# Four attention layers on one core: layers 0 and 1 as one list of steps, two gates where two barriers stood

## The reference, cut to what matters

```python
def _L0(x, mask, kv, kv_mask, ...):        # x: 8 x 256 x 512, 16 heads of 16
    q, k, v = Wq x + bq, Wk kv + bk, Wv kv + bv
    attn = softmax(q k / 4 + mask)
    mean, ex2 = attn @ v, attn @ (v * v)
    std = sqrt(relu(ex2 - mean * mean))
    return (instance_norm(x) * std + mean) * mask
def _L1(x, latents, attention_mask, ...):  # latents: layer 0's result
    h = concatenate([x, latents])          # 512 keys, 256 queries, 16 heads of 32
    q = latents @ q_w + q_b;  k, v = h @ kv_w + kv_b
    o = softmax(q k / 32 + mask) @ v @ out_w + out_b + latents
    return gelu(rmsnorm(o) @ mlp_w1 + mlp_b1) @ mlp_w2 + mlp_b2 + latents
```

## Time and profile before

| | us |
|---|---|
| median of three executions | 3299.74 (3284.89 to 3302.26) |
| the profiled execution | 3297.55 |
| its span in the trace | 3295.8 |
| TensorE busy | 2809.2 |
| VectorE busy | 1824.8 |
| ScalarE busy | 1338.8 |
| GpSimd busy | 881.5 |

### The profile page before, as it was taken

How to read it: one execution, slowest core, us unless ns; L and a number is a source line. 1 busy time by engine, 2 the same in 40 slices (tenths; PEclk the granted TensorE clock), 3 DMA queues, 4 the chain that set the end, 5 groups by cost and what they waited for, 6 DMA issues and landing times. The chain is left out here.

```text
span 3295.8 us, 41359 instructions
## 1 busy us (share of the span) xinstructions
PE 2809.2 (85%) x14624; PEld 1317.3 (40%) x14624; DVE 1824.8 (55%) x4498; ACT 1338.8 (41%) x2342; POOL 881.5 (27%) x722
## 2 busy tenths in 40 slices
PE   4988888867999999989999999985668888888895
PEld 1222222224555555556555545542222333333332
DVE  3777777713433433212555665567867776667641
ACT  0566665642333333322333333322215544554562
POOL 1577777752444444310010000001110010101000
PEclk7999999978999999899999999988678899999997
DMA  4444444320002000122323232333333232323210
GB/s 99 102 100 102 102 99 102 67 95 23 27 30 92 28 27 24 65 63 56 67 53 69 57 70 52 70 63 86 67 82 87 69 76 59 89 52 77 66 34 20
DMA packets 182335, 219.93 MB, mean 67 GB/s; under 512 B 40840, under 2 KB 135664, under 8 KB 175984
## 3 DMA queue, kind: packets, MB, share of 16 engines
q1 hardware_dynamic: 170064, 189.74, 25.0%
q0 software_dynamic: 6016, 20.98, 1.9%
q10 hardware_dynamic: 6048, 6.56, 0.6%
HBM read 146.90 MB, written 51.64 MB: 60 GB/s over the span
## 5 line engine op out<-in xcount | busy, mean ns | idle before, releaser
L1260 DVE TENSOR_REDUCE l_M<-PS 128x1 f32<-128x512 f32 x512 | 330.2, 681 | 168.3 <-PE PS L722 167.9
L1480 DVE TENSOR_REDUCE l_M<-PS 128x1 f32<-128x512 f32 x512 | 334.8, 684 | 139.1 <-PE PS L967 136.2
L1199 ACT ACTIVATE l_P<-PS 128x512 f32<-128x512 f32 x512 | 286.3, 599 | 255.3 <-PE PS L977 237.3
L1563 POOL TENSOR_TENSOR l_S<-l_P 128x512 f32<-128x512 f32 x256 | 326.0, 1305 | 62.0 <-ACT l_P L1050 62.0
L1050 ACT ACTIVATE l_P<-PS 128x512 f32<-128x512 f32 x512 | 276.3, 598 | 134.0 <-PE PS L731 133.5
L967 PE MATMUL PS<-l_KS,l_QS 97*128 97x512 bf16 x512 | 205.4, 412 | 102.9 <-DVE l_M L1480 71.7
L1319 DVE TENSOR_REDUCE l1a_M<-PS 128x1 f32<-128x512 f32 x256 | 158.9, 683 | 201.5 <-PE PS L784 201.5
L1164 ACT ACTIVATE l_P<-l_P 128x1024 f32<-128x1024 f32 x128 | 135.3, 1057 | 304.9 <-DVE l_P L1400 304.7
L1386 DVE CUSTOM_DVE_ANT_0 l_JK<-PS,l_MK 128x256 f32<-128x256 f32 x512 | 195.6, 420 | 102.1 <-PE PS L897 99.9
L722 PE MATMUL PS<-l_KS,l_QS 97*128 97x512 bf16 x512 | 202.5, 406 | 57.7 <-DMA l_KS<-l_MB 19.5
L612 PE MATMUL PS<-l_YT,l_w_mlp_w 128*128 128x256 f32 x1024 | 238.6, 390 | 5.2 <-ACT l_YT L1126 5.1
(11 more groups left out here) (244 smaller groups left out, 4639.8 us busy)
## 6 DMA issues: line engine op xcount, KB each, us to landing
l_QS<-q_scratch SPq DMA_DIRECT2D x128, 128.0 KB, 5.6
q_scratch<-l_T SPq DMA_DIRECT2D x96, 128.0 KB
l_QS<-q_scratch SPq DMA_DIRECT2D x32, 384.0 KB, 5.0
k_scratch<-l_T SPq DMA_DIRECT2D x96, 128.0 KB
l_KS<-k_scratch SPq DMA_DIRECT2D x32, 384.0 KB
l_QS<-q_scratch SPq DMA_DIRECT2D x32, 256.0 KB, 5.6
l_KS<-k_scratch SPq DMA_DIRECT2D x32, 256.0 KB
l_RB<-l_recs SPq DMA_DIRECT2D x32, 256.0 KB
```

Source lines behind the costliest of these rows:

```text
L1199: e.activation(t.P[quad % 4][:, m, :], PS[:, COUNTS.bank[st], :], ACT.Exp, scale=0.25).then_inc(q.sem("act.exp", st), 1)
L1260: e.tensor_reduce(t.M[i % 2][:, qt, hd:hd + 1], PS[:, COUNTS.bank[st], :], AX.X, ALU.max).then_inc(q.sem("dve.smax", st), 1)
L1480: e.tensor_reduce(t.M[i % 2][:, qt, hd:hd + 1], PS[:, COUNTS.bank[st], :], AX.X, ALU.max).then_inc(q.sem("dve.smax", st), 1)
L1563: x = e.tensor_tensor(t.S[j % 2][:, m, :], t.P[2 * j % 4][:, m, :], t.P[(2 * j + 1) % 4][:, m, :], ALU.add)
```

## The change

The two barriers go. `layer0_order` now gives plain places (stage n of item i at beat i + n), layer 1's list begins at `BEGIN1 = 18.35`, and all four layers are sorted into one list. In layer 0's list marks 3 and 4 are set at 17.4 and 19.4; layer 1's list has gate 3 at 17.6 (ScalarE, GpSimd and SyncE wait there, VectorE and TensorE don't) and gate 4 at 19.6 (all but TensorE). `1.start` is split: the weights of keys, queries and values and the value bias come behind gate 3, the output weights, the other bias row and GpSimd's memsets behind gate 4 (`1.start2`). Layer 1's load of the mask becomes a step of its own (`1.mload`), 0.3 beats behind the load of the batch, and the first four maxima of layer 1 are moved back to 1.46 to 1.76. Tiles are given new places, so that what layer 1 uses early lies where layer 0 is through early.

```diff
-    return pipeline((a0, a1, a2, c, p), ((0.0, 1.0),) * 5, keep=True)
+    order = [(2 * b + h + beat + at, st) for b, h in ITEMS for beat, part in enumerate((a0, a1, a2, c, p)) for at, st in part(b, h)]
+    return order + [(-9, ("0.start", 0, 0, 0)), (17.4, ("mark", 3, 0, 0)), (19.4, ("mark", 4, 0, 0))]
+BEGIN1 = 18.35
@@ layer1_order
-            at = -0.9 if b else 0.0
-            out += [(at, k("load")), (at + 0.15, k("mrow"))] + [((0.6 + at) if b else 0.05, k("lat", 0)), ((0.7 + at) if b else 0.08, k("lat", 1))]
+            out += [(-0.9 if b > 1 else -0.7, k("load")), (-0.6 if b else 1.2, k("mload")), (-0.5 if b else 1.27, k("mrow"))]
+            out += [(-0.3 if b else 0.0, k("lat", 0)), (-0.2 if b else 0.03, k("lat", 1))]
...
-        out += [(1.05 + 0.2 * n, k("smax", n)) for n in range(4)] + [(1.8, k("rows")), (1.81, k("turn"))]
+        out += [((1.05 + 0.2 * n) if (b, h) > (0, 0) else (1.46 + 0.1 * n), k("smax", n)) for n in range(4)] + [(1.8, k("rows")), (1.81, k("turn"))]
...
+    return order + [(-0.75, ("gate", 3, 0, 0)), (-0.74, ("1.start", 0, 0, 0)), (1.25, ("gate", 4, 0, 0)), (1.25, ("1.start2", 0, 0, 0)),
+                    (18.95, ("mark", 2, 0, 0))]
@@ tables
-("1.load", "dve"): 0.1,
+("1.mload", "dve"): 0.01,
-GATED = {0: ("pe", "sp", "pool"), 1: ("pe", "sp"), 2: ("pe", "act", "dve", "pool", "sp")}
+GATED = {3: ("act", "pool", "sp"), 4: ("act", "dve", "pool", "sp"), 0: ("pe", "sp", "pool"), 1: ("pe", "sp"), 2: ("pe", "act", "dve", "pool", "sp")}
@@ tensor1, 1.smax
-                q.wait_ge("pool.start", ("1.start", 0, 0, 0))
+                q.wait_ge("pool.start", ("1.start2", 0, 0, 0))
...
+                q.wait_ge("act.exp", ("0.sc", B - 1, 1, 31))
+                q.wait_ge("act.sums", ("0.sout", B - 1, 1, 1))
@@ scalar1
-                for n, x, s in (("k_w1", t.wk, "wk/0"), ("q_w1", t.wq, "wq/0"), ("v_w1", t.wv, "wv/0"), ("out_w1", t.wo, "wo/0")):
+                for n, x, s in (("k_w1", t.wk, "wk/0"), ("q_w1", t.wq, "wq/0"), ("v_w1", t.wv, "wv/0")):
                     weights(q, s, x, n)
+            elif kind == "1.start2":
+                weights(q, "wo/0", t.wo, "out_w1")
@@ vector1
             if kind == "1.start":
                 q.wait_ge("rows", st)
-                e.memset(t.MB[0][:, 256:512], 0.0)
+                e.memset(t.MB[0][:, 256:512], 0.0).then_inc(q.sem("dve.start", st), 1)
+            elif kind == "1.start2":
                 e.memset(t.MB[1][:, 256:512], 0.0).then_inc(q.sem("dve.start", st), 1)
-            elif kind == "1.load":
+            elif kind == "1.mload":
                 q.wait_ge("inm", st)
-                q.next_needs(e.tensor_scalar(t.MF[:, :], t.MI[:, :], 0.0, None, ALU.not_equal))
...
-                e.tensor_scalar(t.MB[b % 2][:, 0:256], t.MF[:, :], -1.0, NEG, ALU.add, ALU.mult).then_inc(q.sem("dve.mask", st), 1)
+                e.tensor_scalar(t.MB[b % 2][:, 0:256], t.MI[:, :], 0.0, -NEG, ALU.is_equal, ALU.mult).then_inc(q.sem("dve.mask", st), 1)
@@ gpsimd1
             elif kind == "1.load":
                 q.wait_ge("pstore", step("1.f2", i - 5))
+                q.wait_ge("store", ("0.f5", b, 1, 1))
...
+            elif kind == "1.mload":
+                q.wait_ge("dve.mask", step("1.mload", i - 2))
                 e.dma_start(t.MI[:, :], I["mask1"][b:b + 1, :]).then_inc(q.sem("inm", st), 16)
@@ sync2: 2.start2 waits for the last weighted sum of layer 1 in place of its last score; 2.lload also for layer 0's store
```

More of the change, by code:

```diff
@@ L14 @@
 NEG = 1e30
-def merge(*lists):
-    placed = []
-    for n, (steps, start, end) in enumerate(lists):
-        for i, s in enumerate(steps):
-            if s is not None and isinstance(s[0], float):
-                placed.append((start + (end - start) * s[0], n, i, s[1]))
-                continue
-            s, delay = s if isinstance(s, tuple) and isinstance(s[1], float) else (s, 0.0)
-            placed.append((start + (end - start) * (i + 0.5) / len(steps) + delay, n, i, s))
-    return [(at, s) for at, _, _, s in sorted(placed, key=lambda x: x[:3]) if s is not None]
-SPANS = ((0.0, 0.9), (0.0, 0.8), (0.05, 0.8), (0.0, 1.0), (0.0, 1.0))
-def pipeline(stages, spans=SPANS, tail=None, keep=False, begin=()):
-    n, order = len(ITEMS), []
-    first = 0 if stages[0] else 1
-    for i in range(first, n + 4):
-        lists = []
-        for s, (f, span) in enumerate(zip(stages, spans)):
-            if f and 0 <= i - s < n:
-                steps = f(*ITEMS[i - s])
-                if steps:
-                    lists.append((steps, *span))
-        if i == n + 3 and keep:
-            return order + [(i, ("barrier", 0, 0, 0))], lists[0]
-        if i == n + 2 and keep:
-            order.append((i, ("mark", -1, 0, 0)))
-        if i == first and tail:
-            order += [(i + at, st) for at, st in merge(*lists, (tail[0], 0.0, 0.8))]
-            order += [(i + 1, ("barrier", 0, 0, 0))] + [(i + 1, st) for st in begin]
-        else:
-            order += [(i + at, st) for at, st in merge(*lists)]
-    return order + [(n + 4, ("barrier", 0, 0, 0))], None
 def layer0_order():
@@ L114, in steps @@
         return out
-    order = sorted([(2 * b + h + at, st) for b, h in ITEMS for at, st in steps(b, h)] + merge((tail[0], 0.0, 0.8)), key=lambda x: x[0])
-    first = lambda x: x[0] < 1 or x[1][0][0] == "0"
-    order = [x for x in order if first(x)] + [(1, ("barrier", 0, 0, 0))] + [x for x in order if not first(x)]
-    return order + [(18.95, ("mark", 2, 0, 0))]
+    order = [(2 * b + h + at, st) for b, h in ITEMS for at, st in steps(b, h)]
+    return order + [(-0.75, ("gate", 3, 0, 0)), (-0.74, ("1.start", 0, 0, 0)), (1.25, ("gate", 4, 0, 0)), (1.25, ("1.start2", 0, 0, 0)),
+                    (18.95, ("mark", 2, 0, 0))]
 BEGIN2 = 16.75
@@ L183, in whole_order @@
 def whole_order():
-    o0, tail = layer0_order()
-    order = [(0, ("0.start", 0, 0, 0))] + o0 + [(0, ("1.start", 0, 0, 0))]
-    rest = [(BEGIN2 + at, st) for at, st in layer2_order()] + [(BEGIN2 + 18.3 + at, st) for at, st in layer3_order()]
-    o1 = layer1_order(tail)
-    n = o1.index((1, ("barrier", 0, 0, 0))) + 1
-    order += o1[:n] + sorted(o1[n:] + rest, key=lambda x: x[0])
+    places = ((0, layer0_order()), (BEGIN1, layer1_order()), (BEGIN1 + BEGIN2, layer2_order()),
+              (BEGIN1 + BEGIN2 + 18.3, layer3_order()))
+    order = sorted([(begin + at, st) for begin, steps in places for at, st in steps], key=lambda x: x[0])
     order += [(99, ("barrier", 0, 0, 0))]
@@ L356, in count @@
                         self.add(total, name, self.slot[name, st], st, 16 * n)
-            if st[0] == "mark" and st[1] < 0:
-                moved = {s: v for s, v in total.items() if "/" in s}
-            elif kind == "mark":
+            if kind == "mark":
                 self.marks.setdefault(st[1], {}).update(total)
             if kind == "barrier":
-                self.barrier.setdefault(st, {}).update({**total, **(moved or {})})
-                uses, moved = {}, None
+                self.barrier.setdefault(st, {}).update(total)
+                uses = {}
         self.total.update(total)
@@ L814, in tensor1 @@
                 if kt == 0:
-                    q.wait_ge("act.vals", step("1.out", i, 0) if g else step("1.out", i - 1, 1))
+                    q.wait_ge("act.vals", step("1.out", i, 0) if g else step("1.out", i - 1, 1) if i else ("0.out", B - 1, 1, 1))
                 q.wait_ge("act.exp", step("1.sc", i, j // 2))
```

86 lines of the change are left out of this document (47 added, 39 removed), and 4 rows, old and new, of tables (LATER, MOVES).

## The result

The changed kernel takes 3281.4 us (median of 12 executions, 3273.5 to 3298.1) against 3299.0 us (12 executions, 3284.9 to 3311.1) for the kernel before: ratio 0.9957, 95% interval 0.9941 to 0.9972. The forecast was 3264 us, 33.6 us less than the profiled execution of before. The ratio gives 14 us (9 to 19), the medians differ by 17.6. The time lies in the wider of the two ranges (3246 to 3288) and just outside the forecast's own (3252 to 3280); about half of the saving came.

A forecast was written before the change was run, and what follows sets the result against it. TensorE was taken to bound the kernel, idle mainly from 657.0 to 788.7 us. With 72.9 us of work and 25.2 of waits, layer 1's first turn comes 33.6 us earlier: 3264 us, range 3252 to 3280 (8 in 10: 3246 to 3288).

The forecast's parts named there:

- 1 gate 3 and bias row: Near 650 us, VectorE's memset waits for the value bias, holding up maxima; TensorE waits 5.2 us.
- 2 rows of maxima: Layer 0's last head-half: TensorE's existing wait for the rows of maxima to land stays, 2.5 us.
- 3 square roots: Layer 0's drain: of TensorE's 4.4 us for exponentials behind ScalarE's square roots, some 1 us is left (0 to 4.4).
- 4 ScalarE in order: Boundary: projection evictions stand before exponentials in ScalarE's list; TensorE waits 6 us in all (0 to 15).
- 5 lower clock: Boundary: two half-clock spells of TensorE, behind the bias-row and maxima-row waits, cost 4.5 us (0 to 10.3).
- 6 gate 4: Behind the gate at 19.6, VectorE's wait for the second mask delays TensorE's first layer 1 maxima by 3 us (0 to 10).
- 7 last normalization: Layer 0's last normalization holds ScalarE and VectorE before layer 1's second maxima and first exponentials; 3 us (0 to 10).
- the second rival: Layer 0's drain stays paced by ScalarE: 47.5 us of waits, 11 saved, 3286 us; chance 0.10.
- stood for a mask behind the turn: Rival: layer 1's mask loads lose their lead, TensorE stands 9 us in seven batches; 29 us slower, 3327; chance 0.07.
- a barrier's: Rival: the gates at the boundary make TensorE wait as barriers did; only 3 us won, 3295 us; chance 0.06.
- a total that moves otherwise than the turn: Sign of a wrong forecast: the whole kernel's time changes differently from layer 1's first turn, forecast 33.6 us earlier.
- the first rival: Everything fits at the boundary: TensorE keeps only 2.5 + 1.3 + some 5 us; 50 us saved, 3248; chance 0.17.

The follow-up runs named there:

- a2: Changed kernel with VectorE's small operations on the maxima (`rows`) of layer 1's first three items ahead of the last value eviction again; 3262.4 us, ratio to before 0.9899.
- a3: Kernel before, with the same small operations of layer 1's first three items moved behind the last value eviction; 3315.8 us, ratio to before 1.0072.
- b1: Changed kernel, with GpSimd's fourth fold of layer 1's items 0 and 1 waiting until VectorE's `rows` is done; 3272.6 us, ratio to before 0.9928.
- a4: Changed kernel, with layer 0's steps of equal place in the order of the kernel before; 3275.5 us, ratio to before 0.9936.
- a1: The changed kernel run again without any edit, for a second profile; 3274.3 us, ratio to before 0.9937.
- b3: Changed kernel, with VectorE's memset and its wait for the value-bias row half a beat later; 3277.4 us, ratio to before 0.9945.
- b2: Changed kernel, second mask issued before the batch's load, which waits for the first mask rows, and output weights half a beat later; 3273.9 us, ratio to before 0.9941.
- d1: c3 with ScalarE's two squares of the means of item (6, 1) 0.11 beats later and the square roots 0.12; 3244.0 us, ratio to before 0.9855.
- c2: Changed kernel with the edits of a2 and b2 together; 3257.4 us, ratio to before 0.9893.
- c3: Changed kernel with a2, b2 and b3 together, plus SyncE's `spread` of item (6, 1) behind the next item's turned maxima rows; 3257.2 us, ratio to before 0.9890.

## Why the prediction failed

**The step that failed stands in the first paragraph**: that layer 1 is bound by TensorE, so that whatever brings its first turn forward brings the end forward by as much. It needs layer 1 to run the same list as before. Besides the mask steps, which the change moves by intent, it didn't, on one engine and for three items: from the first to the fourth turn it took 126.4 us instead of 110.5, and 15.9 of the 19.4 us that the turn came earlier were lost there (a2, a3 and b1 show how). The window could not warn, since it shows the old list. The new list could: it differs from the old one where no edit points. I compared the two orders only around the boundary. The prediction put the new places of tiles at nothing and didn't count the one merged list, with its shifted places, as a part of the change at all.

The end did not follow the turn the other way either: behind layer 2's first turn the profile is 14.8 us shorter than before. Of that stretch the forecast says nothing, and in this pair of profiles nearly the whole gain stands in it (the open ends below; by A + B the front gained 10 to 16 us). So it was in part luck, and not the reasoning, that brought the measured time within 3246 to 3288.

**The turn itself** came 19.4 us earlier and not 33.6. 6.7 of the difference lie ahead of the boundary: the maxima at 643.63 stood at 636.89 in the profile before. Most of that is the spread of single executions (a4 and the profiles behind it). From that event to the turn it took 125.7 us instead of 151.8, so 26.1 were won. In a1 it was 762.24 - 644.15 = 118.1, what 151.8 - 33.6 asks for: of two profiles of this kernel one gave the forecast of the stretch, though not by the forecast's terms (its waits were 2.88, 1.30, 1.76 and, behind gate 4, 4.32 us). Term by term, in the first profile:

| step | forecast | measured |
|---|---|---|
| 1 gate 3 and bias row | 5.2 | 2.75 |
| 2 rows of maxima | 2.5 | 3.04 |
| 3 square roots | 1 | 1.79 |
| 4 ScalarE in order | 6 | 4.2 (the 0.83 at 688.08, 1.09, 0.67, 0.62, 0.96) |
| 5 lower clock | 4.5 | 1.7 + 4.4 + 6.7 = 12.8 |
| 6 gate 4 | 3 | 4.67 + 0.79 = 5.5 |
| 7 last normalization | 3 | 0 |
| not in the forecast: the turn's wait for VectorE's own step `rows` | | 1.4 |

The sum is 31.5 instead of 25.2; the other 1.2 of the 7.5 us missing lie in gaps under half a microsecond and were not traced further. The mis-sized term is the fifth, 12.8 us where 4.5 were forecast and 10.3 was its upper bound. For the spell behind gate 4 I had allowed no time of its own; the stretch from 748.0 to 763.5 ran at a clock of 0.57, that is 86% of it at the lower level, and so about 0.86 x 15.5 / 2 = 6.7 us were lost behind a wait of 4.67. The spell behind the rows of maxima cost 4.4 (a1). The one behind the bias row is short: from 658.66 to 663.00 the mean clock was 0.61, so by the same working about 0.78 x 4.34 / 2 = 1.7 us.

```profile
658.66:663.00 4.34, 4.34 (x16) 1.15 (x17) 2.81 (x5) 0.91 (x2) 0.00 (x0) 0.61 1.02 385
```

Step 7 cost nothing: between 750 us and the turn VectorE has of the normalization only a reciprocal of 0.34 us, and a2, with the same normalization behind the turn, kept TensorE busy all through B.

Step 1: the row landed 3.6 us after its issue at 654.28 and not 7.6; VectorE stood for 4.01 us. In the profile:

```profile
l1a_row_vb<-in_rows SPq DMA_DIRECT2D x1, 256.0 KB, 3.5
```

The row that I had taken as the nearest was not so near: before, the load went out 0.8 us behind the first of the weight loads (708.44 against 707.66), now 0.6 us ahead of it (654.28 against 654.89). So the 3.5 us don't test the rule of the Trainium skill ("DMA: Bandwidth & Descriptors", Queues, rings and completion order) that DMA engines take turns between queues; no run here does. Its 4 us would not have mattered: b3 took the whole wait away, and the next one in line took its place. Step 6: VectorE's second mask, the wait I had priced, ended at 747.85; what TensorE waited for, until 748.08, were the first mask rows, 1 KB transfers for which I had allowed 2 us, though in the profile before they had taken 3.7 (median of the four), and of which the last took 5.8 beside 2 MB (b2). Gate 4 opened 8.4 us after the last weighted sum's end (SyncE issued again at 737.47), 0.9 us later than allowed. Step 4, where I feared most, was right in size, but not as told: there were five waits of 0.6 to 1.1 us and not one beside each projection, and the first stands ahead of the first projection.

One bound was not kept apart: item 1 ends at 7 us in its own text and at 9 in the second rival and in the sum of all high ends. With 7 these two would be 3284 and 3298 instead of 3286 and 3300.

**The rivals.** None was it. TensorE never stood for a mask behind the turn (VectorE waited 10.62 us for the first, until 736.41, and 8.04 for the second, both ahead of the turn), ScalarE didn't pace the drain, and gate 4 cost TensorE one wait of 4.67 us, not a barrier's. The measured time is nearest to the second rival's 3286, but not by its terms: its 9 and 15 us were 2.75 and 4.2. I had named a total that moves otherwise than the turn as what would prove the reasoning wrong, but gave it no chance of its own; this is what came. Nor was everything as good as it could be, as the first rival had it; d1, with 40 us saved in A and B, shows how much more there was.

**Left open**: the last 2 to 3 us of layer 0's ties, and layers 2 and 3. From layer 2's first turn to layer 3's first turn the profiles range from 853 to 877 us (877 before, 864 changed, 853 in c2) with the same list but for a few ties. a3, which has the list of before, took 864 as well, in the fastest of its six executions. So 13 us of the difference between the two first profiles lie there, and whether that is chance or a part of the change (the new places of tiles, the ties) is not shown. The spread hides what a front part gains when a median of five to twelve is read, and is why A and B were read in the profiles.

## What to carry to other kernels

Where an order comes from sorted numbers, a shift of a whole block is no neutral edit: compare the two orders on every engine from end to end, count each exchange as a part of the change, and break ties with integers or an explicit rank. When a wait on a full engine is taken away, look at what it had hidden and follow a late transfer down the list: the wait for the bias row hid the rows of maxima, and these and the squares both stood behind the same late reciprocals. Moving the first two brought A from c2's 123.0 to c3's 121.7 us; only the run that moved the third as well gained, to 116.3. A short operation on the way to TensorE's next input should not meet a long GpSimd operation.
